# One block for a decoder layer: preparation inside the attention's first slots, feed-forward's input ahead of its last, copies of the maxima issued by ScalarE

## The reference

```python
x = x + attn(layernorm(x), Wq, bq, Wk, bk, Wv, bv, Wo, bo)       # softmax(Q K^T / 4) V, then Wo
x = x + xattn(layernorm(x), ctx, ctx, mask, wq, bq, wk, bk, ...)  # where(mask == 0, 1e-9, scores)
h = gelu(layernorm(x) @ absmean(W_fc).T)                          # exact gelu
x = x + (layernorm(h) * ln_w + ln_b) @ absmean(W_proj).T
# absmean(W): gamma = mean(|W|) + 1e-6; sign(W / gamma) * min(round(|W / gamma|), 1)
```

## Time and profile before

| what | value |
|---|---|
| median of 3 runs | 2607.31 us (2600.8 to 2608.62) |
| the profiled execution | 2609.64 us, its span 2607.8 us |
| busy: TensorE, VectorE, ScalarE, GpSimd | 2210.0, 2033.7, 1609.8, 1026.5 us |
| mean granted TensorE clock | 0.963 |
| preparation, attention, feed-forward begin | 0, 56.74, 2016.82 us |
| first feed-forward product | 2033.85 us |

### The profile page before, as it was taken

How to read it: one execution, slowest core, us unless ns; L and a number is a source line. 1 busy time by engine, 2 the same in 40 slices (tenths; PEclk the granted TensorE clock), 3 DMA queues, 4 the chain that set the end, 5 groups by cost and what they waited for, 6 DMA issues and landing times. The chain is left out here.

```text
span 2607.8 us, 72523 instructions
## 1 busy us (share of the span) xinstructions
PE 2210.0 (85%) x29047; PEld 1457.0 (56%) x29047; DVE 2033.7 (78%) x4023; ACT 1609.8 (62%) x2352; POOL 1026.5 (39%) x719
## 2 busy tenths in 40 slices
PE   3367888888889888888988888888865799999999
PEld 3134555555555555555555555555533477777777
DVE  5257888888888888888888888888753588888887
ACT  2245666666666666666666666665532687788776
POOL 0133443433443433344443344343221454555553
PEclk8679999999999999999999999999987899999999
DMA  3356786666677676667767666776431333333332
GB/s 86 67 88 111 125 131 119 121 127 120 123 124 125 121 119 126 118 123 129 123 122 127 118 122 124 122 126 117 82 68 36 67 83 94 97 89 81 95 97 58
DMA packets 450752, 276.75 MB, mean 106 GB/s; under 512 B 299344, under 2 KB 401104, under 8 KB 450512
## 3 DMA queue, kind: packets, MB, share of 16 engines
q1 hardware_dynamic: 447728, 270.68, 55.7%
q10 hardware_dynamic: 2784, 2.43, 0.3%
HBM read 54.87 MB, written 33.55 MB: 34 GB/s over the span
## 5 line engine op out<-in xcount | busy, mean ns | idle before, releaser
L616 ACT ACTIVATE prob<-exp_bank 128x1024 f32<-128x1024 f32 x512 | 523.0, 1022 | 289.2 <-PE exp_bank L870 285.6
L714 DVE TENSOR_REDUCE cross_mx<-score_bank 128x8 f32<-128x1024 f32 x256 | 311.0, 1215 | 136.2 <-PE score_bank L852 136.2
L714 DVE TENSOR_REDUCE self_mx<-score_bank 128x8 f32<-128x1024 f32 x256 | 310.4, 1213 | 135.1 <-PE score_bank L852 135.1
L550 POOL TENSOR_TENSOR xs<-xn,xs 128x1024 f16<-128x1024 f32 x64 | 136.1, 2127 | 686.6 <-ACT xs L643 686.6
L1267 PE MATMUL hbk<-wfcT,ffn_xhl 128*128 128x512 f16 x1024 | 265.5, 383 | 28.5 <-DMA ffn_xhl<-ffn_xs 26.6
L550 POOL TENSOR_TENSOR ahl<-attT,ahl 128x512 f16<-128x512 f32 x128 | 148.0, 1156 | 349.6 <-ACT ahl L621 349.6
L1227 DVE SCALAR_TENSOR_TENSOR ghl<-tbk,lnwc,ghl 128x512 f16<-128x512 f32 x256 | 187.9, 735 | 100.3 <-ACT ghl L1158 100.3
L1243 PE MATMUL ybk<-wpT,ghl 128*128 128x256 f16 x2048 | 260.5, 273 | 0.8 <-DVE ffn_y L1212 0.7
L1243 PEld LDWEIGHTS ybk<-wpT,ghl 128*128 128x128 f16 x2048 | 197.9, 98 | 66.0 <-DVE ghl L1227 0.9
L1158 ACT ACTIVATE ghl<-tbk,lnwc 128x512 f16<-128x512 f32 x256 | 174.0, 680 | 68.3 <-PE tbk L1257 68.3
L746 DVE STREAM_TRANSPOSE out_bank<-out_bank 128x512 f32<-128x512 f32 x256 | 183.9, 718 | 40.3 <-PE out_bank L887 40.3
(11 more groups left out here) (162 smaller groups left out, 4654.9 us busy)
## 6 DMA issues: line engine op xcount, KB each, us to landing
self_stk<-self_qk SPq DMA_DIRECT2D x768, 64.0 KB, 2.4
cross_stk<-cross_qk SPq DMA_DIRECT2D x768, 64.0 KB, 2.4
self_src<-in_x SPq DMA_DIRECT2D x32, 512.0 KB, 5.7
ctx_in<-in_ctx SPq DMA_DIRECT2D x32, 512.0 KB, 6.3
x_scratch<-xn SPq DMA_DIRECT2D x32, 512.0 KB, 5.5
ffn_src<-x_scratch SPq DMA_DIRECT2D x32, 512.0 KB, 3.8
out<-ffn_y SPq DMA_DIRECT2D x32, 512.0 KB, 3.6
self_stk<-self_negmT SPq DMA_DIRECT2D x64, 128.0 KB, 3.8
```

Of the source, the lines that this page charges most:

```text
L550: nc.gpsimd.tensor_tensor(out, src, hi, ALU.subtract).then_inc(lo_ready, 1)
L616: act.activation(prob[:, p % 3], ebank[:, :, :], ACT.Exp, scale=EXP_SCALE).then_inc(b.exp_done, 1)
L714: dve.tensor_reduce(a.mx[:, 8 * m:8 * m + 8].rearrange("p (j r) -> p r j", r=2), sbank[:, :, :].rearrange("p r (j k) -> p r j k", j=4), AX ...
```

## The change

The three parts get one block. The preparation becomes a set of pieces that are placed between the attention's slots: x and context are loaded first; the eight matrices are turned before slot 3 (counted from 0, two per step), mask tables and ternary weights are made between slots 3 and 6, the cross chain's constants before slot 6. The first projection waits for `w_lo` at 8, the first sum with `boB` for `bo_done`. LayerNorm's two tables come from one product series instead of two, and ScalarE copies the turned projection weights. The feed-forward's first loads and its first normalisation (`mlp...(-1)`) stand on every engine ahead of slots 72 and 73, the attention's last; they wait for 31 of the 32 stores. The two DMAs of the maxima go from SyncE, behind the stacking, to ScalarE, behind the copy that they read. The hardware loops of the attention become straight code on all engines.

```diff
 def decoder_layer_kernel(nc, ins, out):
     x2_dram = nc.dram_tensor("x2_scratch", (B, S, D), F32, kind="Internal").ap()
-    with ExitStack() as stack:
+    with ExitStack() as stack, nc.Block() as block:
         sb, _, _ = allocators(nc, stack, stack)
         sh = Shared(sb)
-        setup(nc, stack, ins, sh)
-        attention(nc, stack, ins, sh, x2_dram)
-        ffn(nc, stack, sh, x2_dram, out)
+        prep = setup(nc, stack, ins, sh)
+        att = attention(nc, stack, ins, sh, x2_dram, prep)
+        mlp = ffn(nc, stack, sh, x2_dram, out, att)
+        LAST = 2 * (NG + 4)
+        @block.sync
+        def _(sp):
+            att.load_first(sp)
+            prep.load_weights(sp)
+            att.slots(lambda s: att.sync(sp, s), 0, 3)
+            att.await_primed(sp, 1)
+            att.slots(lambda s: att.sync(sp, s), 3, 5)
+            att.await_primed(sp, 2)
+            att.slots(lambda s: att.sync(sp, s), 5, 8)
+            att.await_primed(sp, 8)
+            att.slots(lambda s: att.sync(sp, s), 8, LAST)
+            mlp.load_first(sp)
+            mlp.sync(sp, -1)
+            att.slots(lambda s: att.sync(sp, s), LAST, LAST + 2)
+            mlp.unrolled(sp, lambda i: mlp.sync(sp, i))
+            mlp.await_stores(sp)
+        @block.gpsimd
+        def _(pool):
+            prep.constants(pool)
+            att.slots(lambda s: att.gpsimd(pool, s), 0, 2)
+            att.slots(lambda s: att.gpsimd(pool, s, prep.bo_done), 2, 3)
+            att.slots(lambda s: att.gpsimd(pool, s), 3, LAST)
+            mlp.gpsimd(-1)
+            att.slots(lambda s: att.gpsimd(pool, s), LAST, LAST + 2)
+            mlp.steps(pool, mlp.gpsimd)
+        @block.scalar
+        def _(act):
+            prep.load_small(act)
+            att.slots(att.scalar, 0, 3)
+            prep.weights_high(act)
+            att.slots(att.scalar, 3, 4)
+            prep.magnitudes(act)
+            att.slots(att.scalar, 4, 6)
+            prep.projection_out(act)
+            att.slots(att.scalar, 6, LAST)
+            mlp.scalar(-1)
+            att.slots(att.scalar, LAST, LAST + 2)
+            mlp.steps(act, mlp.scalar)
+        @block.vector
+        def _(dve):
+            att.slots(att.vector, 0, 2)
+            att.prime_queries(dve, 0, prep.consts)
+            prep.mask_parts(dve)
+            att.prime_queries(dve, 1, prep.consts)
+            prep.weights_low(dve)
+            att.slots(att.vector, 2, 4)
+            att.prime_values(dve)
+            prep.ternary(dve)
+            prep.tables(dve)
+            att.slots(att.vector, 4, 6)
+            prep.ternary_out(dve)
+            prep.tables_out(dve)
+            att.prime_cross(dve)
+            att.slots(att.vector, 6, LAST)
+            mlp.vector(-1)
+            att.slots(att.vector, LAST, LAST + 2)
+            mlp.steps(dve, mlp.vector)
+        @block.tensor
+        def _(pe):
+            prep.turn_weights(pe)
+            att.slots(att.tensor, 0, 4)
+            prep.mask_products(pe)
+            att.slots(att.tensor, 4, 6)
+            prep.turn_ternary(pe, att.maxima_out, att.exp_done)
+            prep.table_products(pe)
+            prep.await_tables(pe)
+            att.slots(att.tensor, 6, LAST + 2)
+            mlp.steps(pe, mlp.tensor)
...
+        ORDER = (SQ, SK, SO, XO, SV, XQ, XK, XV)
...
+        def load_weights(sp):
+            for n, w in enumerate(ORDER):
+                sp.dma_start(wnat[:, w], ins.weights[w].rearrange("(m p) i -> p m i", p=P)).then_inc(w_in[n], 16)
+            sp.dma_start(fnat[:, 0], ins.Wfc.rearrange("(t p) d -> p t d", p=P)).then_inc(f_in, 16)
+            sp.dma_start(fnat[:, 1], ins.Wp.rearrange("(t p) h -> p t h", p=P)).then_inc(f_in, 16)
+            sp.dma_start(lnb_col[:, :], ins.lnb.rearrange("(t p) -> p t", p=P), allow_slow_non_contiguous=True).then_inc(lnb_in, 16)
+        def load_small(act):
+            act.dma_start(imask[:, :], ins.mask[0, 0]).then_inc(mask_in, 16)
+            for n, b in enumerate(ins.qk_biases):
+                act.dma_start(bcol[:, n], b.rearrange("(m p) -> p m", p=P), allow_slow_non_contiguous=True).then_inc(bias_in, 16)
+            for n, b in enumerate(ins.v_biases):
+                act.dma_start(bv_col[:, n * KT:(n + 1) * KT], b.rearrange("(m p) -> p m", p=P), allow_slow_non_contiguous=True).then_inc(bias_in, 16)
+            for n in range(2):
+                act.dma_start(boB[:, n], ins.o_biases[n].partition_broadcast(P)).then_inc(bias_in, 16)
+            act.dma_start(sh.lnwc[:, :], ins.lnw.rearrange("(t p) -> p t", p=P), allow_slow_non_contiguous=True).then_inc(lnw_in, 16)
...
+        def turn_weights(pe):
+            pe.wait_ge(consts, 2)
+            for n, w in enumerate(ORDER):
+                pe.wait_ge(w_in[n], 16)
+                for mt in range(KT):
+                    for kt in range(KT):
+                        last = nc.tensor.transpose(bank[:, TURN[n], kt * D + mt * P:kt * D + (mt + 1) * P],
+                                                   wnat[:, w, mt, kt * P:(kt + 1) * P], ident[:, :])
+                last.then_inc(w_T, 1)
+            pe.wait_ge(bv_split, 2)
+            pe.wait_ge(w_lo, 4)
...
+        def weights_high(act):
+            for n, w in enumerate(ORDER):
+                act.wait_ge(w_T, n + 1)
+                nc.scalar.activation(WT[:, w, HI], bank[:, TURN[n], :].rearrange("p (k o) -> p k o", k=KT),
+                                     ACT.Copy, scale=WS).then_inc(w_hi, 1)
+            act.wait_ge(scaled, 1)
...
+        def weights_low(dve):
+            dve.wait_ge(bias_in, 16 * 8)
...
+            for n, w in enumerate(ORDER):
+                dve.wait_ge(w_hi, n + 1)
+                nc.vector.scalar_tensor_tensor(WT[:, w, LO].rearrange("p k o -> p (k o)"), bank[:, TURN[n], :], WS,
+                                               WT[:, w, HI].rearrange("p k o -> p (k o)"),
+                                               ALU.mult, ALU.subtract).then_inc(w_lo, 1)
+            dve.wait_ge(bo_mm, 1)
+            nc.vector.scalar_tensor_tensor(boB[:, :, :].rearrange("p n d -> p (n d)"), bank[:, 0, :], 1.0 / WS,
+                                           boB[:, :, :].rearrange("p n d -> p (n d)"), ALU.mult, ALU.add).then_inc(bo_done, 1)
...
+        def ternary(dve):
...
+            dve.wait_ge(m_mm, 1)
...
+            dve.wait_ge(total_done, 1)
...
+        def turn_ternary(pe, maxima_out, exp_done):
+            pe.wait_ge(tern_done, 2)
+            pe.wait_ge(maxima_out, 1)
+            pe.wait_ge(exp_done, 8)
...
+        def magnitudes(act):
+            act.wait_ge(f_in, 32)
+            for n in range(2):
+                nc.scalar.activation(neg[:, n], fnat[:, n], ACT.Abs, accum_out=asum[:, n:n + 1]).then_inc(abs_done, 1)
+        def projection_out(act):
+            for to in (wpT32, wpT):
+                for half in range(2):
+                    act.wait_ge(pj_T, half + 1)
+                    nc.scalar.activation(to[:, 4 * half:4 * half + 4, :].rearrange("p (a t) d -> p a (t d)", a=2),
+                                         bank[:, PROJECTION[half]:PROJECTION[half] + 2, :], ACT.Copy).then_inc(pj_out, 1)
...
+        def table_products(pe):
+            pe.wait_ge(lnb_done, 1)
+            pe.wait_ge(fc_out, 2)
+            for t in range(FT):
+                if t % 4 == 0:
+                    pe.wait_ge(pj_out, t // 4 + 1)
+                last = nc.tensor.matmul(bank[:, 2, 0:D], lnB[:, t], wpT32[:, t], start=(t == 0), stop=(t == FT - 1))
+            last.then_inc(c2_mm, 1)
+        def await_tables(pe):
+            pe.wait_ge(pj_out, 4)
+            pe.wait_ge(c2_done, 1)
...
+        def slots(program, first, last):
+            for n in range(first, last):
+                i = n // 2 - 2
+                program(Slot(crs, slf, i - 2, i, i, i) if n % 2 else Slot(slf, crs, i, i - 3, i, i + 1))
...
-            def maxima():
-                if s.ga is not None:
-                    sp.wait_ge(a.mT_out, s.ga + 1)
-                    for r in range(2):
-                        sp.dma_start(a.stk[HALF * r + STACK:HALF * (r + 1), s.ra, 0].rearrange("p j k t -> p (j k) t"),
-                                     a.negmT[:, :].unsqueeze(1).broadcast_to([H, FT // 2 * KT, T])).then_inc(a.m_in, 16)
             turn_context()
             stacks(0)
             stacks(1)
             turn_input()
...
+            def maxima_rows():
+                if s.ga is not None:
+                    act.wait_ge(a.mT_out, s.ga + 1)
+                    for r in range(2):
+                        act.dma_start(a.stk[HALF * r + STACK:HALF * (r + 1), s.ra, 0].rearrange("p j k t -> p (j k) t"),
+                                      a.negmT[:, :].unsqueeze(1).broadcast_to([H, FT // 2 * KT, T])).then_inc(a.m_in, 16)
...
             maxima_in()
+            maxima_rows()
             split_outputs(b, s.gb, 0)
...
+                    if s.gq == 0 and not b.cross:
+                        pe.wait_ge(prep.w_lo, 8)
...
```

(40 more changed lines are left out.)

394 lines of the change are left out of this document (148 added, 246 removed).

## The result

The changed kernel takes 2616.38 us (median of 5 runs, 2615.01 to 2617.22), the kernel before 2601.41 beside it: ratio 1.0049, interval 1.0032 to 1.0066. Forecast was 2540. The profiled execution took 2617.22 us with a span of 2615.4, against 2609.64.

What follows compares the result with a forecast made beforehand. Handovers were taken to pace the attention, with no engine full, and TensorE to bound the feed-forward; 2609.64 - 38.8 (head) - 12 (steady) - 18.5 (join) = 2540.3, predicted 2540 us, range 2500 to 2582.

Steps and rivals of the forecast that it cites:

- Steady: 12 us saved: Steady attention: moving the maxima's DMAs to ScalarE saves 12 us, 9 in cross slots and 3 in self slots.
- 28 cross slots give 26.0 - 28 x 0.6 = 9 us: Cross slots: 26.0 us of waits for maxima removed, less 0.6 per slot as GpSimd's ahl blocks VectorE's product.
- In self slots ... I take 3: Self slots: context transpose starts up to 1.24 us later, so of 16.3 us of waits only 3 are gained.
- stacking DMAs that land later since maxima now move beside them: Steady stage's lower bound: maxima's bytes slow the stacking DMAs in every slot, 25 to 31 us lost.
- rival 2: Crowded DMAs: maxima beside the last stacking DMAs delay the landing the next scores wait for; 2580 us, chance 0.18.
- Rival 3: Slower than before: ScalarE's issues lie wholly on every slot's path, 71 us lost; 2623 us, chance 0.05.
- forecast 38.8: Head: preparation under the first slots saves 50.8, less 2 before the first scores and 10 before slot 6.
- The gain of 50.8 at the first product: Head: first projection starts at 24 us instead of 74.81, 50.8 us saved.
- DMA issues on SyncE ... delay nothing: Head: SyncE's issues of loads, large matrices and one row are over by 10 us and cost nothing.
- Loops made straight, costed at nothing: Attention loops: straight code costs nothing since code is fetched ahead; if it were not, 13 us.
- forecast 18.5: Join to the feed-forward: early first input removes the 24 us hole, less 4.9 and 0.6; 18.5 us saved.
- the term "4.9": Join: ScalarE's early-input work ahead of slot 72 delays its exponentials, so the last slots end 4.9 us later.

Runs made afterwards that it cites:

- e13: Changed kernel with seven matmuls that nobody reads ahead of the wait for the stacks in cross slots: 2587.49 us, ratio 0.9939 to the kernel before.
- e1: Changed kernel with the maxima's two DMAs issued by SyncE again, behind the last stacking DMAs; rest as changed: 2557.53 us, ratio 0.9814 to the kernel before.
- e9: e1 with ScalarE also issuing two tiny DMAs (rows of 32 bytes) where the change issues the maxima: 2572.01 us, ratio 0.9874 to the kernel before.
- e10: e9 with the two further DMAs in full, 128 KB each, to a scratch in DRAM: 2638.49 us, ratio 1.013 to the kernel before.
- e4: Changed kernel with a third, tiny DMA issued by ScalarE behind the maxima's two, TensorE waiting for it too: 2672.41 us, ratio 1.0277 to the kernel before.
- e11: e6 with the first eight of each slot's 24 stacking DMAs issued by GpSimd instead of SyncE: 2485.72 us, ratio 0.9543 to the kernel before.
- e12: e11 with the maxima's DMAs issued by ScalarE again, as in the change: 2546.04 us, ratio 0.9781 to the kernel before.
- e5: e1 without the feed-forward's early input, its work again behind the attention's last slot: 2568.19 us, ratio 0.9875 to the kernel before.
- e6: e1 with VectorE's and ScalarE's parts of the early input moved inside slot 72 instead of ahead of it: 2547.97 us, ratio 0.9785 to the kernel before.
- e8: e1 with ScalarE waiting for its own copy of the maxima but issuing no DMA: 2556.03 us, ratio 0.9817 to the kernel before.
- e2: Kernel before with only the maxima's DMAs moved to ScalarE, loops kept: 2666.74 us, ratio 1.0246 to the kernel before.

## Why the prediction was wrong

The steady stage, slot by slot. I worked these means out from the timelines, over all slots between 200 and 1850 us. A slot runs from the end of one copy of maxima to that of the next. "Wait" is TensorE's wait for stacking DMAs before the first scores. "Falls" is the number of slots in which tile 2's six matmuls took over 1.8 us (1.47 at the full clock); in each of them the granted clock was below full. For the changed kernel these are 20 falls in 28 slots behind self-attention's maxima; the expectation of e13 has 18 in 27.

```
            behind self's maxima        behind cross's maxima      pair
            us     wait   falls         us     wait   falls        us
before      27.16  0.98    1 of 29      29.20  0.38   0 of 29     56.37
e1          27.22  1.07    3 of 28      29.16  0.30   0 of 29     56.39
e9          27.35  1.28    2 of 28      29.34  0.31   2 of 29     56.69
e10         28.17  2.03    8 of 28      30.05  0.85   3 of 28     58.22
changed     29.04  2.36   20 of 28      29.38  0.98   3 of 28     58.42
e4          28.42  2.37    9 of 27      31.24  1.24  16 of 28     59.66
e13         27.74  0.83    0 of 28      29.74  1.21   7 of 29     57.49
e11         26.36  0.24    0 of 28      28.12  0.00   0 of 28     54.48
e12         26.80  0.95    0 of 28      29.49  0.03   7 of 28     56.29
```

**Part 2, "Steady: 12 us saved": wrong, 58 lost.** The steps, as the prediction put them:

- "28 cross slots give 26.0 - 28 x 0.6 = 9 us": none came, 0.2 us a slot was lost. The term behind 0.6 was right in kind: in the changed kernel VectorE's product `ue<-ew,cntL` takes 1180 ns on average (302 before), `nmean` 170, both as forecast; but 0.9 us are lost there, not 0.6. What I mis-sized is the delay in front of it. I took "1.24 if they cost what SyncE pays", where two issues took 1.50 on average, and charged the slot only with the 0.6 of the block. But the product itself now waits 1.36 us for ScalarE's weights (39.5 over 29; 0.34 before), which also stand behind the issues. That the low half of tile 0 and tile 2 move by all of it, and by as much as the wait for negmT had been worth, is my reading: e9 shows that exchange, and in e12 slots of this kind take 29.49 against 28.12 in e11, of which 7 falls of the clock (31.19 against 28.92) are some 0.6 a slot.
- "In self slots ... I take 3": 1.9 us a slot was lost instead. The later transpose of the context costs little: in e9 the transpose starts as late as in the changed kernel (6.67 us behind the copy, against 6.80, and 5.32 in e1), and the slot is 27.35. What matters is the landing of the last stacking DMAs. They are issued later (SyncE is through 2.51 us behind the copy, in e1 2.07) and land later (5.26 against 3.97), and the first scores begin at 5.30, in e1 at 4.02.
- That is the bound I named, "stacking DMAs that land later since maxima now move beside them", at 25 to 31 us lost. The mechanism was right, and I placed it in rival 2 with 0.18. I gave its size from the bytes alone, and left out what a longer wait does to TensorE. In 20 of 28 slots the granted clock fell behind it. In the changed kernel slots of this kind with a slow tile 2 last 29.70 us, the others 27.39; of the other kind 31.21 and 29.16. That is 20 x 2.31 + 3 x 2.05 = 52 us; the rest, (27.39 + 29.16 - 56.39) x 28 = 4 us, is landing and lateness. The split overstates, since the slow slots are also those with the longest wait (2.55 us on average, the others 1.87). e13, which fills the wait and leaves landing and ScalarE alone, gives back 29, though the clock still falls in 7 slots of the other kind (31.45 us against 29.20). So at least half of the loss is the clock, and by the count of slots most of it. The length of this wait doesn't decide it alone: in e4 it is 2.37 us as well, with 9 falls in 27 slots. It isn't shown how the rest divides between SyncE's slower issues, the landing and ScalarE, and no run has the maxima's bytes early without an issue on ScalarE.

The Trainium skill, "TensorE: Matmul & The Clock Gate", section "Part 1: The HAM clock gate (the "warmup" mystery)", says that the chip sets TensorE's clock by how busy it has been, and that a kernel with gaps runs part of its work at the lower level. The traces agree: 0.59 of full behind a wait of 2.51 us. The prediction looked at the clock only at the join, as worth up to 2 us.

The Trainium skill, "DMA: Bandwidth & Descriptors", section "Issuing engines are not separate DMA queues", says that DMAs of all issuers interleave on the same engines. The traces agree: with the bytes on ScalarE's queue the first scores wait 2.03 us for SyncE's stacks (e10), without them 1.28 (e9). It adds that the issue time, all that a second issuer saves, is usually small relative to the DMA. Here it counts: a stacking issue took SyncE 0.68 us on average and landed 2.4 us after its start (median), and eight issues moved from SyncE to GpSimd gave 62 us (e11).

**Rival 3 came true in its number** (2623; 2616.38 measured) and only half in its mechanism. I gave it 0.05, because ScalarE is busy only 953.65 of 1512 us. That is the average share; at the end of a slot four things stand in a row behind the issues. Two issues cost 1.24 us at the least, 1.50 on average and 2.05 in the slot shown.

**Part 1, forecast 38.8, measured 34.8 and 33 (e5).** The gain of 50.8 at the first product is 50.5, but by luck: the two branches came in the opposite order. The weights, forecast to end at 24.6, end at 21.98, since the last of the biases lands at 14.27 and not at 18. The turned x, forecast at 20.9, is there at 24.23, and TensorE waits 2.50 us for it. The step "DMA issues on SyncE ... delay nothing" was wrong: the DMA transpose of x took 8.50 us from issue to landing (4.40 before, issued at 70.36), beside the two 1 MB loads of the feed-forward's weights, which land at 19.56 and 22.11. GpSimd's first `rstd` stands on the same branch: it took 3.00 us beside a copy of VectorE's (1.03 before), and ScalarE's normalising waited for it until 10.33.

At the first maximum of slot 6 38.7 are left (105.32 against 144.03), as forecast. The missing 4 us are lost behind it, up to the mark at 203.46: that stretch takes 98.1 us, 94.2 before. In e1, e5, e6, e8 and e9, where SyncE issues the maxima, it takes 95.5 to 96.8, so part of the 4 is part 2's and 1.3 to 2.6 us are lost without it, for a cause that stays open.

**Loops made straight, costed at nothing: right** (e1 against before, e2 against the changed kernel).

**Part 3, forecast 18.5, measured 16.2.** The hole of 23.85 us before the first product is gone, the feed-forward's products follow directly. The error is in the term "4.9". Timelines of VectorE, ScalarE and TensorE after the change:
```profile
2005.03 1.41 DVE L1344 BATCH_NORM_STATS2 ffn_stats<-ffn_src 128x6 f32<-128x256 f32 x4 [6.06 <-DMA ffn_src<-x_scratch]
...
2009.79 1.28 DVE L845 TENSOR_TENSOR ue<-exp_bank,ew 128x512 f32<-128x512 f32 x2
```
```profile
2008.46 2.07 ACT L1282 ACTIVATE ffn_xn<-ffn_src,ffn_nmr,ffn_rstd 128x256 f32<-128x256 f32 x4 [7.74 <-DVE ffn_nmr L1332]
```
```profile
2011.21 1.04 PE L946 MATMUL exp_bank<-maskBT,pick 64*128 64x512 bf16 x4 [10.66 <-DVE ue L845]
...
2035.94 5.30 PE L1031 MATMUL product_bank<-WT,ahl 128*128 128x256 f16 x24 [4.80 <-POOL ahl L654]
2041.03 1.31 PE L1379 MATMUL hbk<-wfcT,ffn_xhl 128*128 128x512 f16 x5
```
I looked at ScalarE's queue and not at VectorE's. VectorE waits 6.06 us for the load, with the `ue` of slot 72 behind it in its order, and TensorE waits 10.66 for `ue`. The last shifted scores start 12.07 us behind the copy of the maxima, 5.09 before: 7.0 lost, not 4.9. In e1 it is 15.22 us of waiting, because SyncE issues the 31st store only behind the maxima:
```profile
1941.57 2.17 SPq L643 DMA_DIRECT2D cross_stk<-cross_negmT  x2
1943.79 0.59 SPq L637 DMA_DIRECT2D x_scratch<-xn  x1
1948.20 0.92 SPq L1390 DMA_DIRECT2D ffn_src<-x_scratch  x2
```
So the early input is worth less there; e6, with VectorE's part behind its first outputs, gets back 9.6.

**What e11 adds.** In e1 the chain that ended last was 44% SyncE's issues. In e11 it reads (shares of the span by engine):
```profile
PE 42%; DVE 31%; issue 11%; ACT 5%; SPq 5%; DMA 3%; POOL 3%; DVEq 0%; POOLq 0%; ACTq 0%
```
The queue of 24 stacking issues, some 16 us of every slot, had been the longest link. The change took two issues from that queue, 1.24 us, and gave them to an engine with less slack at that place; e11 takes eight issues and gives them to the one that idles some 11 us in that part of the slot:
```profile
970.05 4.03 POOL L599 DMA_DIRECT2D cross_stk<-cross_qk  x8 [2.42 <-ACT cross_qk L733]
```

## What to carry to other kernels

Ask of a removed wait not only how long it was but what it covered: here the waits for maxima covered two issues on ScalarE, which cost 14 us beside them (e9); with the waits gone and the maxima's bytes moved as well they cost 60 (e12). Where a transfer is moved to start earlier, look for the transfer it will move beside and for the engine that waits for that one; if this is TensorE, price a longer wait with the clock behind it, not only with its own length. Issue DMAs from the engine that idles at that moment by the timeline, not from the one whose average share is low, and read each in-order queue for what stands behind a new wait.

## What was new of the hardware

- Waits of TensorE of some 2.4 us, in a stage where it is busy 87% of the time, were followed in 20 of 28 cases by a fall of the granted clock (0.59 of full over 3.5 us in the slot shown). Seven matmuls of no use in that wait removed all 20 falls behind self-attention's maxima and saved 29 us. In e12 the seven falls follow another wait of TensorE, 1.8 to 2.6 us for VectorE's low half ahead of tile 2.
- Two DMA issues on ScalarE took 1.24 to 2.36 us, 1.50 on average. The last eight stacking issues on SyncE took 5.9 us on average in e1 and 6.3 in the changed kernel, where ScalarE's DMAs moved beside them. Eight on GpSimd took 4.03 in the slot shown, 0.51 each on average in e11 against SyncE's 0.71.
- A DMA transpose issued beside two 1 MB loads took 8.50 us to land, 4.40 without them.
- A DMA of one row of 128 bytes costs ScalarE no less to issue than one of 128 KB (e4: 0.6 to 2.3 us; the maxima's in the changed kernel: 0.6 to 1.7).
